# A four-layer graph network on one core: aggregations of layers 2 and 3 by row halves, and three steps written in another order

## What is computed

```python
x = layernorm(x + gnn0(x, adj))     # two projections, sum over neighbours
x = layernorm(x + gat_ffn(x, adj))  # 4 heads, elu, one output head, elu, FFN of two products, norm
x = layernorm(x + gat2(x, adj))
x = layernorm(x + gat3(x, adj))
```

```python
Wh = x @ W
logits = leaky_relu((Wh @ a_src)[:, :, None] + (Wh @ a_dst)[:, None, :], 0.2)
logits = where(adj == 0, -inf, logits)
out = nan_to_num(softmax(logits, axis=-1)) @ Wh
```

## Time and profile before

| | |
|---|---|
| median of 3 runs | 3140.3 us (3139.85 to 3141.08) |
| the profiled execution | 3139.89 us |
| its span, first to last instruction | 3138.2 us |
| mean granted clock of TensorE | 0.993 of full speed |
| steps 3 and later of the loop | from about 2251 us to the end |

### The profile page before, as it was taken

One profiled execution on the slowest core, in us unless ns is written; L12 is line 12 of the kernel. 1 busy time (PEld: TensorE's weight loads), 2 busy tenths in 40 slices (PEclk: granted clock), 3 DMA queues, 4 the chain that ended last, 5 costly groups with the idle time before them and its releaser, 6 DMA issues.

```text
span 3138.2 us, 64986 instructions
## 1 busy us (share of the span) xinstructions
PE 3074.8 (98%) x19593; PEld 2691.9 (86%) x19593; DVE 2297.8 (73%) x4825; ACT 1776.1 (57%) x4325; POOL 2061.9 (66%) x2773
## 2 busy tenths in 40 slices
PE   8999989999999999999999999999899999999997
PEld 6888878889988888898889889888688888888885
DVE  6777656777777776777777777765788888888886
ACT  3333335555555555555555555543577777777775
POOL 5666635666666666666666656641688888888886
PEclk9999999999999999999999999999899999999999
DMA  6555411111111111111111111114332333223220
GB/s 198 178 190 177 151 46 40 41 50 50 47 53 40 53 40 55 45 47 53 47 47 40 60 40 47 53 41 155 91 97 82 100 94 97 86 91 100 90 74 28
DMA packets 181766, 244.46 MB, mean 78 GB/s; under 512 B 15808, under 2 KB 81344, under 8 KB 181696
## 3 DMA queue, kind: packets, MB, share of 16 engines
q1 hardware_dynamic: 169920, 218.46, 21.5%
q10 hardware_dynamic: 9216, 16.78, 1.4%
q0 software_dynamic: 2560, 8.39, 0.8%
HBM read 159.68 MB, written 83.89 MB: 78 GB/s over the span
## 4 chain that ended last, share of the span: by engine, by line
PE 76%; issue 5%; POOL 3%; ACT 1%; DVE 1%; DMA 0%; SPq 0%; POOLq 0%; ACTq 0%; DVEq 0%
PE wop L2020 23%; PE hp L2006 20%; PE wop L47 9%; PE hp L2171 5%; PE hp L47 5%; PE agg L1989 4%; PE shared L2028 2%; PE agg L2131 2%; PE shared L2131 2%; POOL w_first L1223 1%; PE shared L248 1%; PE hp L2158 1%; POOL g_terms L1291 1%; PE smallp L200 1%; POOL cols L389 0%
## 5 line engine op out<-in xcount | busy, mean ns | idle before, releaser
L1223 POOL TENSOR_TENSOR w_first<-xd,v_row 128x512 f32<-128x512 f32 x480 | 682.5, 1435 | 346.1 <-DMA xd<-x_scratch 315.3
L2006 PE MATMUL hp<-yT_hi,big_hi 128*128 128x256 f32 x2048 | 595.1, 291 | 0.0
L2006 PE MATMUL hp<-yT_hi,big_lo 128*128 128x256 f32 x2048 | 580.1, 283 | 0.0
L2006 PE MATMUL hp<-yT_lo,big_hi 128*128 128x256 f32 x2048 | 579.8, 283 | 0.0
L2020 PE MATMUL wop<-big_hi,hT_hi 128*128 128x512 f32 x1024 | 424.8, 415 | 0.4 <-ACT v_row L1404 0.4
L2020 PE MATMUL wop<-big_hi,hT_lo 128*128 128x512 f32 x1024 | 402.1, 393 | 0.0
L2020 PE MATMUL wop<-big_lo,hT_hi 128*128 128x512 f32 x1024 | 400.5, 391 | 0.0
L2006 PEld LDWEIGHTS hp<-yT_hi,big_hi 128*128 128x128 f32 x2048 | 392.8, 192 | 7.5 <-DVE yT_lo L1698 0.7
L2006 PEld LDWEIGHTS hp<-yT_lo,big_hi 128*128 128x128 f32 x2048 | 392.7, 192 | 3.0 <-issue 0.2
L2006 PEld LDWEIGHTS hp<-yT_hi,big_lo 128*128 128x128 f32 x2048 | 392.7, 192 | 0.0
L1291 POOL TENSOR_TENSOR g_terms<-x,g_v_row 128x512 f32<-128x512 f32 x256 | 368.1, 1458 | 35.3 <-ACT x L1557 33.5
(11 more groups left out here) (218 smaller groups left out, 8115.2 us busy)
## 6 DMA issues: line engine op xcount, KB each, us to landing
x0f<-in_x_turned SPq DMA_DIRECT2D x64, 256.0 KB, 2.7
xt<-in_x SPq DMA_DIRECT2D x64, 256.0 KB, 2.9
x_scratch<-w_first ACTq DMA_DIRECT2D x64, 256.0 KB, 2.2
xa<-x_scratch SPq DMA_DIRECT2D x64, 256.0 KB, 2.7
att_hi_scratch<-att_hi SPq DMA_DIRECT2D x64, 256.0 KB, 2.0
att_lo_scratch<-who SPq DMA_DIRECT2D x64, 256.0 KB, 2.0
att_scratch<-attT SPq DMA_DIRECT2D x64, 256.0 KB, 2.0
att_hi<-att_hi_scratch SPq DMA_DIRECT2D x64, 256.0 KB, 3.7
```

The source lines that it names most:

```text
L1223: nc.gpsimd.tensor_tensor(terms[:, k % TR, :], xd[:], v_row[:, k, :], ALU.mult).then_inc(terms_ready, 1)
L2006: ins = nc.tensor.matmul(hp[half][:, s * 2 * P:(s + 1) * 2 * P], a, b, start=c == 0 and i == 0, stop=c == KC - 1 and i == 2)
```

## The change

Five things:

1. `aggregate3` takes each of its four matmuls as two, one for each graph: 64 rows as the stationary side, 64 columns of `turned` as the moving side, each graph into a bank of its own. `turned` shrinks to 64 columns, and `pool_zero` is gone.
2. The banks are dealt out anew: `g2` sums into the first halves of both banks of `agg`, `g3` into the second halves, `g2`'s small results go to `shared`. For this the aggregations wait for both layers' low parts.
3. ScalarE: layer 3's exponent stands ahead of `h1_hi`; layer 2's norm stands ahead of both dots of layer 2 (it stood between them). VectorE: layer 3's `after_exp` stands ahead of `h1_lo`.
4. GpSimd: the first product of layer 3 stands ahead of layer 2's diagonal, the second behind it.
5. The last two output sums of layer 1 take the form by halves too (`last_sums`), and the last exponent, ELU and rounding move from the end of step 2 to the middle, ahead of layer 2's first copies and its first aggregation.

```diff
@@ SlotAttention
-        self.turned = piece(6 * NODES, P)
+        self.turned = piece(6 * NODES, NODES)
...
-            nc.scalar.copy(self.turned[r, :, r], self.turned_psum[r, :, r]).then_inc(self.turned_ready, 1)
+            nc.scalar.copy(self.turned[r, :, :], self.turned_psum[r, :, r]).then_inc(self.turned_ready, 1)
@@ banks
-            agg_2, agg_3 = (bank.rearrange("p (c n) -> p c n", c=KC) for bank in (agg[:, 0, :], shared[:]))
-            small_2, small_3 = agg[:, 1, :], smallp[:]
+            agg_2, agg_3 = (agg[:, :, q * KC * NODES:(q + 1) * KC * NODES].rearrange("p g (c n) -> p g c n", c=KC)
+                            for q in range(2))
+            small_2, small_3 = shared[:], smallp[:]
@@ ScalarE
-                    nc.scalar.copy(g.aggS[0][:], g.agg[:]).then_inc(g.agg_hi_ready, 1)
+                    nc.scalar.copy(by_graph(g.aggS[0][:]), g.agg).then_inc(g.agg_hi_ready, 1)
...
+                    if isinstance(n, int) and n == 2:
+                        last_exp(T - 1)
+                        split_att(T - 1, PAIRS)
                     if live(n, 2):
                         turned3(g2, n - 2)
...
@@ TensorE
+                def last_sums(s, j):
+                    pe.wait_ge(ao_.turned_ready, 2 * s + 2)
+                    for c in range(KC):
+                        for b in range(2):
+                            own = slice(b * NODES, (b + 1) * NODES)
+                            ins = nc.tensor.matmul(agg_2[:, b, c, :], who[j][own, c * P:(c + 1) * P],
+                                                   ao_.turned[own, 0, own], start=True, stop=True)
+                    ins.then_inc(uo_done, 1)
+
                 def aggregate3(g, t, x):
                     pe.wait_ge(g.att.turned_ready, 2 * t + 2)
-                    ge(pe, g.agg_lo_ready, t)
                     for c in range(KC):
-                        ins = nc.tensor.matmul(g.agg[:, c, :], x[:, c * P:(c + 1) * P], g.att.turned[:, 0, :],
-                                               start=True, stop=True)
+                        for b in range(2):
+                            own = slice(b * NODES, (b + 1) * NODES)
+                            ins = nc.tensor.matmul(g.agg[:, b, c, :], x[own, c * P:(c + 1) * P],
+                                                   g.att.turned[own, 0, :], start=True, stop=True)
                     ins.then_inc(g.agg_done, 1)
...
                     if live(n, 5):
+                        pe.wait_ge(g2.agg_lo_ready, capped(n - 2, T))
+                        ge(pe, g3.agg_lo_ready, n - 5)
                         aggregate3(g3, n - 5, x3[(r - 5) % R])
...
                     if live(n, 2):
+                        if isinstance(n, int) and n == 2:
+                            pe.wait_ge(att_ready, T)
+                        if live(n, 5):
+                            pe.wait_ge(g3.agg_lo_ready, n - 4)
+                        ge(pe, g2.agg_lo_ready, n - 2)
                         aggregate3(g2, n - 2, x2[(r - 2) % R])
```

More of the change, by code:

```diff
@@ L347, in act_turned @@
         act.wait_ge(self.turned_done, t + 1)
-        if isinstance(t, int) and t == 0:
-            act.wait_ge(self.zeroed, 1)
         for g in range(2):
             r = slice(g * NODES, (g + 1) * NODES)
-            nc.scalar.copy(self.turned[r, :, r], self.turned_psum[r, :, r]).then_inc(self.turned_ready, 1)
+            nc.scalar.copy(self.turned[r, :, :], self.turned_psum[r, :, r]).then_inc(self.turned_ready, 1)
 class SlotNorm:
@@ L1010, in gnn_stack_kernel @@
             g3 = Gat("g3", 3 * KC, agg_3, small_3, wop[1], g3_own, 256, g3_rows, g3_terms, g3_agg, g3_z)
-            g2.wide, g3.wide = wop, (wop[1], shared)
+            g2.wide, g3.wide = wop, (wop[1], smallp)
             weights = (w1, w2, W2, W3)
@@ L1033, in run, with by_graph, turned_att @@
                     step(p)
+            def by_graph(x):
+                return x.rearrange("p c (g n) -> p g c n", g=2)
+            def turned_att():
+                return attT[:].rearrange("p (c g n) -> p g c n", c=KC, g=2)
             def pair(p):
@@ L1321, in step3 @@
                             products3(g2, n - 1, k, x2[(r - 1) % R][:], x2_ready)
+                    if live(n, 3):
+                        products3(g3, n - 3, 0, x3[(r - 3) % R][:], g2.x_ready)
+                    if live(n, 1):
                         diag3(g2, n - 1)
                     if live(n, 3):
-                        for k in range(2):
-                            products3(g3, n - 3, k, x3[(r - 3) % R][:], g2.x_ready)
+                        products3(g3, n - 3, 1, x3[(r - 3) % R][:], g2.x_ready)
                     if isinstance(n, int) and n == 2:
@@ L1388, in keep_wo, with last_exp @@
                     nc.scalar.copy(who[j][:], wop[j][:]).then_inc(who_ready, 1)
+                def last_exp(s):
+                    act.wait_ge(uo_done, s + 1)
+                    act.wait_ge(att_stored, 16 * s)
+                    nc.scalar.activation(turned_att(), agg_2, ACT.Exp).then_inc(exo_ready, 1)
                 def out_exp(s):
@@ L1639, in step3 @@
                     if live(n, 1):
+                        dot3(g2, n - 1, 0)
                         dot3(g2, n - 1, 1)
-                    if isinstance(n, int) and n == 2:
-                        out_exp(T - 1)
-                        split_att(T - 1, PAIRS)
                     if isinstance(n, int) and n == 3:
@@ L1667, in _ @@
                 ao_.act_exp(nc, act, 2 * m + 1)
-                out_exp(2 * m)
+                last_exp(2 * m)
                 keep_att(1)
@@ L1739, in out_elu @@
                     dve.wait_ge(nego_ready, s + 1)
+                    if isinstance(s, int) and s >= T - 2:
+                        nc.vector.tensor_tensor(turned_att(), agg_2, turned_att(), ALU.max).then_inc(att_ready, 1)
+                        return
                     nc.vector.tensor_tensor(attT[:], shared[:], attT[:], ALU.max).then_inc(att_ready, 1)
@@ L1843, in agg_lo @@
                     dve.wait_ge(g.agg_hi_ready, t + 1)
-                    nc.vector.tensor_tensor(g.aggS[1][:], g.agg[:], g.aggS[0][:].bitcast(F32), ALU.subtract
-                                            ).then_inc(g.agg_lo_ready, 1)
+                    nc.vector.tensor_tensor(by_graph(g.aggS[1][:]), g.agg, by_graph(g.aggS[0][:].bitcast(F32)),
+                                            ALU.subtract).then_inc(g.agg_lo_ready, 1)
                 def scores(g, t):
@@ L1926, in step3 @@
                         after_exp(g2, n - 2)
+                    if isinstance(n, int) and n == 2:
+                        out_elu(T - 1)
                     if live(n, 4):
@@ L1934, in step3 @@
                         g2.norm.dve_mean(nc, dve, n - 3, g2.x_ready)
+                    if live(n, 4):
+                        after_exp(g3, n - 4)
                     if live(n, -2):
                         h1_lo(n + 2, r + 2)
-                    if live(n, 4):
-                        after_exp(g3, n - 4)
                     if live(n, 2):
@@ L1944, in step3 @@
                         g3.norm.dve_mean(nc, dve, n - 5, g3.x_ready)
-                    if isinstance(n, int) and n == 2:
-                        out_elu(T - 1)
                     if isinstance(n, int) and n == 3:
@@ L2216, in step3 @@
                         pe.wait_ge(att_ready, T - 1)
-                        out_sums(T - 1, 1)
+                        last_sums(T - 1, 1)
                     if isinstance(n, int) and n == 3:
-                        pe.wait_ge(att_ready, T)
                         spread_rows(g3)
@@ L2246, in _ @@
                 first_half(2, 2)
-                out_sums(2 * m, 0)
+                pe.wait_ge(y_lo_ready, 8 * PAIRS)
+                last_sums(2 * m, 0)
                 pe.wait_ge(ao_.turned_ready, 2 * (2 * m + 1))
```

12 lines of the change are left out of this document (3 added, 9 removed).

## The result

| | before | changed |
|---|---|---|
| median of 4 runs each, same chip | 3140.07 us | 3195.14 us |
| lowest and highest | 3139.69 to 3141.08 | 3189.75 to 3197.99 |
| the profiled execution, its span | 3139.89, 3138.2 us | 3193.89, 3192.2 us |
| one step of the steady stretch | 14.10 us | 14.95 us |

The ratio is 1.0173, with a 95% interval of 1.0155 to 1.019: 55.1 us more, where 43.9 were forecast. The time lies inside the range of 3172 to 3200 us, near its upper end.

A forecast was written before the change was run, and what follows sets the result against it. The prediction took TensorE's own instructions, without waits, as the bound. To 3140.3 us it added 43.1 for 56 steps, 0.8 for one more, +2 at the start and -2 at the end: 3184 us, range 3172 to 3200.

The forecast's parts named there:

- Slots don't follow the columns: Aggregations of layers 2 and 3: a pair of half-row loads still takes 0.11 us with 64 moving columns.
- the two rivals for faster: Aggregations: slots follow the columns, 0.056 us a pair, 3132 or 3139 us, chance 0.07; whole block halves, 3097 us, chance 0.02.
- the prediction's rival of 3097 us: Aggregations: the whole block halves with no price at its ends, -0.89 us a step from the blocks; chance 0.02.
- The blocks: TensorE's aggregations by row halves: layer 2's grows by 0.35 us, layer 3's by 0.29 us, 0.64 us a step.
- The 0.05 us for the last pair: End of each aggregation: only the last pair gains, half a slot, since behind it nothing loads.
- The wait for GpSimd's diagonal: TensorE ahead of layer 2's 64-column pair: waits 0.13 us a step, up to 0.43.
- the sentence that layer 3's diagonal comes earlier: GpSimd, behind layer 2's diagonal: layer 3's diagonal comes earlier, not later; no size given.
- the sign that I named for this wait: View of waits: should name GpSimd's diagonal ahead of the 64-column pair in most steps, 0.1 to 0.2 us each.
- The steady sum: The 56 steps of the steady stretch: 56 x (0.64 + 0.13) = 43.1 us more.
- The start: Before the steady stretch: first aggregation of layer 2 comes 2.4 us later, taken as +2 us (0 to +3).
- the step at 2251: The one step at 2251 us, ahead of the 56 counted: adds 0.8 us.
- The end: From 3055 us on, the step bound through GpSimd, which loses idle time: -2 us (-4 to +2).

The follow-up runs named there:

- e4: Kernel before, aggregations over all 128 rows, with 64 moving columns in place of 128 in layers 2 and 3: 3142.56 us, +0.2 over before.
- e5: Changed kernel with an aggregation's two loops exchanged, four column blocks of one graph, then four of the other: 3261.38 us, +117.9 over before.
- e2: Changed kernel with parts 3 and 4 (the new orders on ScalarE, VectorE, GpSimd) taken back: 3181.94 us, +39.6 over before.
- e11: Kernel before with the new orders on ScalarE and VectorE only, GpSimd's order as it was: 3152.19 us, +9.9 over before.
- e3: Changed kernel with GpSimd writing layer 2's diagonal ahead of both products of layer 3: 3185.87 us, +43.5 over before.
- e6: Changed kernel with layer 3's aggregation ahead of layer 2's 64-column pair on TensorE: 3184.64 us, +41.1 over before.
- e7: As e6, but layer 3's aggregation split, two column blocks ahead of layer 2's 64-column pair and two behind: 3202.39 us, +58.9 over before.
- e12: Changed kernel with an aggregation's instructions in groups of four, the graphs taking turns: 3200.03 us, +57.2 over before.
- e8: Kernel before with only layer 3's exponent and reciprocal moved ahead of the FFN's rounding copy and low half: 3141.25 us, -1.1 over before.
- e1: Kernel before with parts 3 and 4 (the new orders on ScalarE, VectorE, GpSimd) alone: 3152.11 us, +9.8 over before.

## Why the prediction was right, and where it wasn't

- **Slots don't follow the columns**: right. The pairs stand 0.11 us apart in the changed kernel, and e4 shows the same on all rows. With that the two rivals for faster fell. The Trainium skill's page "TensorE: Matmul & The Clock Gate" ("LDWEIGHTS (loading the stationary operand)") has a load's time go by its columns and not its rows; the trace agrees, with 0.11 us also for the loads that go alone on half of the rows (e5). The table under "Theoretical Speedup" in the Trainium skill's "TensorEngine Tiling (Array Packing)" gives up to twice the speed for a dimension of 64 or less. Read rightly it isn't contradicted: 16 instructions on halves go in 8 slots, which is twice as fast as one behind the other. But the form over all rows needs 8 slots too, so nothing of it is left to gain here, and the prediction's rival of 3097 us took the table for a gain over that form.
- **The blocks**, 0.35 and 0.29 us: layer 2's went from 1.35 to 1.70 us (median 1.695), layer 3's, from the pair's second matmul, from 1.29 to 1.58. Right; e2's step of +0.62 us is their sum of 0.64, less the 0.02 of the wait that was there before. The 0.05 us for the last pair is there in the form by halves (1.70 against 1.75 in the earlier trace rows), but my reason for it isn't: by it e4 should have gained, and it did not. What fits both is that the passage back waits for the last matmuls themselves; no run varied that.
- **The wait for GpSimd's diagonal**, 0.13 us a step: this is the term of the step that was too small; 0.85 - 0.62 = 0.23 us was measured. The chain came out at the end I took: copies 0.80, norm to 1.63, product 1.72 to 3.02, diagonal to 3.27 us; then 0.12 us to the load, where I had 0.18 to the matmul. The first matmul is late by 0.07 to 0.16 us, 0.12 on average, as forecast. What I left out is the 0.10 us of the pair's second load that no matmul covers once TensorE has stood still. The mechanism was right, but the sentence that layer 3's diagonal comes earlier (5.20 us behind the transposition, 5.63 before) was true only with the product where the change puts it: e11 shows how close the second chain is. And the sign that I named for this wait did not come: the view of waits has it as "issue", not as GpSimd's diagonal. It is the order of time that shows it.
- **The steady sum**: at layer 2's aggregation at 2265.74 us the changed kernel is 3.58 us behind (2269.32), at the one at 3055.38, 56 steps on, 50.76 (3106.13). That is 47.2 us against 43.1.
- **The start**, +2 and the step at 2251 +0.8: 3.6 us against 2.8. The first aggregation of layer 2 moved from 2216.52 to 2219.14 us, 2.6 later (2.4 forecast), with TensorE idle for 4.50 us ahead of it. Behind it the clock was 0.50 from 2220 to 2225 us, where it was 1.00 before.
- **The end**, -2: wrong, +3.2 us from that last aggregation of the earlier trace rows to the end. The idle time of GpSimd that I counted as gained shortened no step: the next three aggregations of layer 2 follow at 13.05 to 13.06 us, where it was 12.94 to 13.00. From the last tile's transposition of the FFN's input to the end the changed kernel takes 2.9 us more (3123.22 to 3192.2, against 3072.15 to 3138.2). Both traces have the same chain of waits there, and its two longest pieces, TensorE's last two projections of layer 3 with what is around them, are these before:

```profile
3121.73 5.72 issue
...
3128.59 5.13 issue
```

and these in the changed kernel:

```profile
3173.21 6.73 issue
...
3181.07 6.67 issue
```

2.55 us longer, with the same twelve matmuls in each, while the clock was at 0.50 of full speed (1.2 GHz) for most of them. The matmuls themselves are the whole of it: 5.19 and 4.51 us for twelve, against 4.17 and 3.02. In the changed kernel TensorE had been idle ahead of them for 2.45 and 1.40 us, in the kernel before for 2.49 and 1.40; yet there the clock fell for a shorter time. This is not one odd execution: from layer 3's last but one transposition to the end e3, e6, e7 and e12 take 24.3 to 24.9 us, the changed kernel 24.6, and before 22.0; but e2, by halves too, takes 22.0. I had counted TensorE's end as a matter of waits and not looked at the clock in the earlier trace rows, which has 0.96 for that stretch.

The span's +54.0 us are 3.6 for the start, 47.2 for the 56 steps and 3.2 for the end, where 2.8, 43.1 and -2 were forecast. All three errors point the same way, and half of them is the end, whose bounds (-4 to +2) left the measured 3.2 out. The time is in the range because the bounds of the steady step were wide enough for all three.

## What to carry to other kernels

Price a matmul by what paces it: where each one loads a new 128-column stationary side, fewer moving columns buy nothing, and taking half of the rows only pays if it lets two different things go at once; two halves of the same work need the same slots plus a passage there and back. Before work is put ahead of a step on another engine, measure the spare time at every point where that engine releases the bound one, here 1.41 us from the diagonal's end to the matmul at layer 2's pair but only 0.21 at layer 3's (5.63 and 5.83 us), of which a matmul that really waits needs up to 0.13; and count a released load as open, not as covered. An order that is harmless by itself (e8) and one that uses up the last tenths (e1, e11) look alike in a diff.

## What the runs showed of the hardware

- A passage from the full array to halves of the rows and back costs 0.29 us beside a 64-column pair and 0.35 between 512-column matmuls (e7; blocks of the changed kernel). It goes with the passages, not with the number of instructions: e7 has those of e6 and takes 17.8 us more.
- Loads on different halves of the rows need not be neighbours to go in parallel. With eight of one half ahead of eight of the other, the spacing fits a ninth that ran beside the fifth (e5: 2.19 us over a block); groups of four cost one short distance, 1.75 us (e12). That a load starts up to four instructions ahead of its turn is what both runs agree with; no run has groups of another size between these.
- A load that waited for GpSimd's diagonal started 0.12 to 0.13 us after its end at layer 2's pair (e1, the changed kernel), and 0.05 or 0.13 us after it at layer 3's (e11). The next load behind it lies open: 0.155 to 0.16 us between a pair's matmuls in place of 0.055.
- The changed kernel's four runs lie within 8 us, the four of before beside them within 1.4. In the start and the end, where TensorE has gaps, the granted clock stood at 0.50 in different places of the traces of nearly equal kernels, and longer in the end of those by halves (mean 0.88 to 0.95 over 74 us, 0.98 over all rows).
